# Blocks of eight tokens in place of a scan over 512: the recurrent layers of a four-layer kernel on one core

## The reference

```python
def step(s, rkvw):                      # s is 16 x 16 for each head
    r_t, k_t, v_t, w_t = rkvw
    a = k_t[..., :, None] * v_t[..., None, :]
    out = jnp.einsum('bhi,bhij->bhj', r_t, u * a + s)
    s = a + w_t[..., :, None] * s
    return (s, out)
...
_, out = jax.lax.scan(step, s0, rkvw)   # over 512 tokens
m = og.mean(-1, keepdims=True)          # og: out by heads
va = ((og - m) ** 2).mean(-1, keepdims=True)
og = ((og - m) / jnp.sqrt(va + 1e-05)).reshape(b, l, e) * gn_w + gn_b
x1 = x + og * g @ Wo.T
```

## Time and profile before

| | us |
|---|---|
| median of 3 runs | 4790.81 (4787.45 to 4797.15) |
| the profiled execution, its own time | 4800.18 |
| its span, first to last instruction | 4798.4 |
| TensorE matmul busy | 3797.2 |
| VectorE busy | 3378.0 |
| ScalarE busy | 2119.3 |
| GpSimd busy | 2302.9 |

### The profile page before, as it was taken

The page is one execution under the profiler, slowest core; times in us unless marked ns, Lnnn a source line. Parts: engine busy times, 40 slices in busy tenths (PEclk is TensorE's granted clock), DMA queues, the critical chain, the costliest instruction groups (busy, mean ns, idle before and its releaser), DMA issues. The chain is left out here.

```text
span 4798.4 us, 50379 instructions
## 1 busy us (share of the span) xinstructions
PE 3797.2 (79%) x15616; PEld 2145.1 (45%) x15616; DVE 3378.0 (70%) x5559; ACT 2119.3 (44%) x4624; POOL 2302.9 (48%) x2245
## 2 busy tenths in 40 slices
PE   7888976867888897686788889768668888877766
PEld 4455732424545573252454546234245454623424
DVE  5677379697667738969665773896966577388696
ACT  5576422413657732231365773223137477322313
POOL 4544455354454545535345454543534544454363
PEclk9999977888999998788899999878889999987888
DMA  3123111101212311110121221011022122201102
GB/s 124 39 80 88 53 44 44 44 27 70 70 42 75 88 53 44 49 39 27 70 70 46 74 85 61 36 53 35 27 76 67 49 75 80 77 20 53 35 27 79
DMA packets 95226, 275.38 MB, mean 57 GB/s; under 512 B 25936, under 2 KB 26704, under 8 KB 73808
## 3 DMA queue, kind: packets, MB, share of 16 engines
q1 hardware_dynamic: 94928, 271.84, 17.7%
HBM read 201.49 MB, written 4.19 MB: 43 GB/s over the span
## 5 line engine op out<-in xcount | busy, mean ns | idle before, releaser
L1282 POOL TENSOR_TENSOR prod<-state,rT 128x512 f32<-128x512 f32 x512 | 698.2, 1367 | 662.1 <-DVE state L1060 605.3
L775 POOL TENSOR_SCALAR probs<-probs,row_inv 128x512 f32<-128x512 f32 x1024 | 693.7, 694 | 639.5 <-DVE row_inv L690 639.5
L1060 DVE TENSOR_TENSOR_SCAN state<-decay,s,kvp 128x512 f32<-128x512 f32 x512 | 911.6, 1782 | 12.7 <-POOL prod L1282 12.7
L634 ACT ACTIVATE probs<-probs,row_max 128x512 f32<-128x512 f32 x1024 | 733.3, 725 | 131.2 <-DVE row_max L706 130.0
L529 PE MATMUL ps<-ident,probs 128*128 128x128 f32 x4096 | 605.4, 289 | 172.2 <-ACT pT L628 145.6
L529 PEld LDWEIGHTS ps<-ident,probs 128*128 128x128 f32 x4096 | 476.7, 146 | 382.5 <-ACT pT L628 209.6
L339 PE MATMUL ps<-mix,wring 128*128 128x512 f32 x1024 | 591.6, 677 | 4.8 <-DMA wring<-in_blocks_dram 4.8
L1197 ACT ACTIVATE state<-s 128x1 f32<-128x1 f32 x512 | 102.0, 202 | 1062.2 <-POOL prod L1282 1062.2
L906 PE MATMUL ps<-vstack,pick 128*128 128x512 f32 x512 | 373.7, 732 | 177.0 <-DVE kvp L1052 177.0
L628 ACT ACTIVATE pT<-ps 128x512 f32<-128x512 f32 x768 | 429.8, 603 | 107.8 <-PE ps L529 107.2
L504 PE MATMUL ps<-kstack,qstack 96*128 96x512 f32 (+1 forms) x1024 | 381.6, 467 | 16.8 <-DMA qstack<-hi 7.0
(11 more groups left out here) (142 smaller groups left out, 6526.2 us busy)
## 6 DMA issues: line engine op xcount, KB each, us to landing
wring<-in_blocks_dram SPq DMA_DIRECT2D x151, 1024.0 KB, 5.0
qstack<-hi SPq DMA_DIRECT2D x256, 64.0 KB, 2.0
kstack<-hi SPq DMA_DIRECT2D x256, 64.0 KB, 2.0
maskA<-in_mask_dram SPq DMA_DIRECT2D x9, 1024.0 KB, 7.5
rows<-in_rows_dram SPq DMA_DIRECT2D x8, 1024.0 KB, 4.5
qstack<-hi SPq DMA_DIRECT2D x256, 32.0 KB, 2.0
qstack<-lo SPq DMA_DIRECT2D x128, 64.0 KB, 2.0
kstack<-lo SPq DMA_DIRECT2D x128, 64.0 KB, 2.0
```

Source lines behind the costliest of these rows:

```text
L634: nc.scalar.activation(p, p, ACT.Exp, bias=row_max[:, n % PSLOTS, qc:qc + 1], scale=-1.0, accum_out=row_sum[:, n % PSLOTS, qc:qc + 1]).the ...
L775: nc.gpsimd.tensor_scalar(p, p, row_inv[:, (n - 1) % PSLOTS, qc:qc + 1], 1.0, ALU.mult, ALU.mult)\
L1060: nc.vector.tensor_tensor_scan(state[:, u % 3, 1:L + 1], decay[:, ug, :], kvp[:, u % 3, :], s0[:, ug, uj:uj + 1], ALU.mult, ALU.add)\
L1282: nc.gpsimd.tensor_tensor(prod[:, t % PRODS, :], state[:, t % 3, 0:L], rT[:, hg % 2, :], ALU.mult)\
```

## The change

The 512-step scans are replaced by blocks of 8 tokens. Inside a block the pairs of tokens (earlier s, later t) are handled in levels of 1, 2 and 4: at each level r and k are first multiplied by the decays that lie between (`k2`, `r2`, `k4`, `r4`, `k8`), the products r*k of a pair are summed over a head by a matmul with `head_sum` (`pair_sums`), multiplied by v on VectorE (`bonus`) and added into the output bank through a matmul with `centre`, which takes the mean over the head away. Per block, `fresh_state` forms sum k v on TensorE, 64 matmuls of 32x32 weights and 128 columns for each group; `other` and `states` bring it to SBUF as [P, 64 blocks, 16]; 16 scans over 63 blocks give the state at each block's start. `spread` writes these states block-diagonally (half of the heads on ScalarE, half on VectorE, in two halves of the tokens), and `from_state` multiplies them by r, 64 matmuls of 32 columns of weights and 128 columns. The values are centred when they are turned to tokens, so the output needs no centring. Variance, power, weight and gate are done for each group while the next one is in work; the power (`inverse_root`) is on GpSimd, 128x512 elements for each group. `wo` accumulates group by group in four banks.

```diff
-                    nc.vector.tensor_tensor(kvp[:, t % 3, :], kT[:, hg % 2, :], ps[:, t % 4, :], ALU.mult)
-                    nc.vector.tensor_tensor_scan(state[:, u % 3, 1:L + 1], decay[:, ug, :], kvp[:, u % 3, :],
-                                                 s0[:, ug, uj:uj + 1], ALU.mult, ALU.add)
...
-                nc.gpsimd.tensor_tensor(prod[:, t % PRODS, :], state[:, t % 3, 0:L], rT[:, hg % 2, :], ALU.mult)
...
+            for hg in range(C):
+                values_to_tokens(hg)
+                pair_sums(hg, 0)
+                pair_sums(hg, 1)
+                middle(hg, 0)
+                if hg > 0:
+                    tokens_to_y(hg - 1)
+                pair_sums(hg, 2)
+                keys_to_tokens(hg)
+                if hg > 0:
+                    variance(hg - 1)
+                fresh_state(hg)
+                pair_sums4(hg)
+                bonus_low(hg)
+                middle(hg, 1)
+                bonus_high(hg)
+                tile = from_state(hg, 0, None)
+                middle(hg, 2)
+                from_state(hg, 1, tile)
+            wo(0)
+            tokens_to_y(C - 1)
+            wo(1)
+            variance(C - 1)
+            gate(C - 1)
+            wo(2)
+            wo(3)
...
+            def fresh_state(hg):
...
+                for tc in range(C):
+                    for r in range(4):
+                        rows_ = slice(32 * r, 32 * r + 32)
+                        for q in range(4):
+                            out = ps[32 * q:32 * q + 32, r, :].rearrange('p (two t x) -> p two t x', two=2, t=C)[:, :, tc, :]
+                            m = nc.tensor.matmul(out, k_tok[rows_, tc, 32 * q:32 * q + 32],
+                                                 v_blocks[rows_, tc, q, :, :, :].rearrange('p two b j -> p two (b j)'),
+                                                 start=True, stop=True)
...
+            def from_state(hg, half, tile):
...
+                for tc in (2 * half, 2 * half + 1):
+                    for b4 in range(4):
+                        for q in range(4):
+                            g32 = 4 * tc + q
+                            m = nc.tensor.matmul(tile[32 * q:32 * q + 32, tc * P:(tc + 1) * P],
+                                                 r_blocks[:, 512 * b4 + 32 * g32:512 * b4 + 32 * g32 + 32],
+                                                 state_bd[:, 4 * g32 + b4 - NB // 2 * half, :],
+                                                 start=(b4 == 0), stop=(b4 == 3), skip_group_check=True)
...
+                for j in range(HS):
+                    ins = nc.vector.tensor_tensor_scan(entry[:, 1:NB, j], w8[:, hg, 0:NB - 1], fresh[:, 0:NB - 1, j],
+                                                       s0c[:, hg, j:j + 1], ALU.mult, ALU.add)
...
+            for hg in range(C):
+                pair_products(hg)
+                for level in range(3):
+                    bonus(hg, level)
+                if hg > 0:
+                    variance_out(hg - 1)
+                bonus(hg, 4)
+                states(hg)
+                spread(hg, 0)
+                if hg > 0:
+                    normalise(hg - 1)
+                if hg == C - 1:
+                    gated(0)
+                spread(hg, 1)
...
+            def inverse_root(hg):
+                pool.wait_ge(*dve_emptied.when('var', l, hg))
+                power = rstdT[:, :].rearrange('p (a b) -> p a b', b=32)
+                nc.gpsimd.tensor_tensor(power, power, minus_half[:, :].unsqueeze(1).to_broadcast([P, L // 32, 32]), ALU.pow)\
+                    .then_inc(*pool_done.reach('rstdT', l, hg))
+
+            for hg in range(C):
+                decays(hg)
+            for c in range(C):
+                add_xa('g', c)
+            for hg in range(C):
+                first_entry(hg)
+                if hg > 0:
+                    inverse_root(hg - 1)
             pool_w(pool, f'o_{l}')
+            inverse_root(C - 1)
             pool_w(pool, f'fk_{l}')
```

More of the change, by code:

```diff
@@ L180, in build @@
-    prod, at = place('prod', [P, PRODS, L], at)
-    recT, at = place('recT', [P, C, L], at)
-    assert over <= at
-    gT, at = place('gT', [P, C, L], at)
[L184 to L189, removed]
+    low_z = at
+    ffn_w, at = place('ffn_w', [P, 2, 2, C * H], at, F32R)
@@ L853, in pe_rwkv, with gate @@
                 mixing('g', c)
[L855 to L862, removed]
+            y_bank = ps[:, OBANK, :]
+            def gate(c):
+                if c == 0:
                     w_wait(pe, f'g_{l}')
-                tile = take(pe, 'gp', l, c) if fc == 0 else tile
-                to_T(pe, tile, weights(f'g_{l}'), mix[:, MIX_AT['g']], c, fcs=(fc,),
-                     fin=tile_ready.reach('gp', l, c) if fc == C - 1 else None,
+                to_T(pe, take(pe, 'gp', l, c), weights(f'g_{l}'), mix[:, MIX_AT['g']], c, fin=tile_ready.reach('gp', l, c),
@@ L867, in gate @@
                      ready=(lambda fc: mix_wait(pe, l, 'g', fc)) if c == 0 else None)
-                return tile
[L870 to L883, removed]
@@ L896, in pe_rwkv @@
[L896 to L921, removed]
@@ L922, in pe_rwkv, with values_to_tokens @@
[L922 to L931, removed]
+            def values_to_tokens(hg):
+                pe.wait_ge(*act_emptied.when('vp', l, hg))
+                tile = take(pe, 'vt', l, hg)
+                for tc in range(C):
+                    m = nc.tensor.matmul(tile[:, tc * P:(tc + 1) * P], vT[:, hg % 2, tc * P:(tc + 1) * P], centre[:, :],
+                                         start=True, stop=True)
+                m.then_inc(*tile_ready.reach('vt', l, hg))
@@ new lines, in pair_sums, with pair_sums4 @@
+            def pair_sums(hg, level):
+                if level == 0 and hg > 0:
+                    pe.wait_ge(*dve_done.when('fresh', l, hg - 1))
+                pe.wait_ge(*dve_done.when('rk', l, hg, level))
+                bank, src = ((0, rk0[:, :]), (1, rk1[:, :]), (2, rk2[:, :, :, :]))[level]
+                nc.tensor.matmul(ps[:, bank, 0:256 if level == 1 else 512], head_sum[:, :], src, start=True, stop=True)\
+                    .then_inc(*tile_ready.reach('sums', l, hg, level))
+            def pair_sums4(hg):
+                pe.wait_ge(*dve_done.when('rk', l, hg, 4))
+                for part in range(2):
+                    nc.tensor.matmul(take(pe, 'sums4', l, hg, part), head_sum[:, :], rk4[:, 2 * part:2 * part + 2, :, :],
+                                     start=True, stop=True).then_inc(*tile_ready.reach('sums4', l, hg, part))
@@ new lines, in bonus_low @@
+            def bonus_low(hg):
+                if hg > 0:
+                    pe.wait_ge(*act_done.when('yT', l, hg - 1))
+                pe.wait_ge(*dve_emptied.when('sums', l, hg, 2))
+                nc.tensor.matmul(y_bank, centre[:, :], rk0[:, :], start=True, stop=False, skip_group_check=True)
+                nc.tensor.matmul(y_bank.rearrange('p (b two) -> p b two', two=2)[:, :, 1], centre[:, :], rk1[:, :],
+                                 start=False, stop=False, skip_group_check=True)
+                by4 = y_bank.rearrange('p (b two t) -> p b two t', two=2, t=2)
+                for s in range(2):
+                    m = nc.tensor.matmul(by4[:, :, 1, :], centre[:, :], rk2[:, s, :, :], start=False, stop=False,
+                                         skip_group_check=True)
+                m.then_inc(*S['context_ready'].reach('low', l, hg))
@@ new lines, in bonus_high @@
+            def bonus_high(hg):
+                by8 = y_bank.rearrange('p (b two t) -> p b two t', two=2, t=4)
+                for s in range(4):
+                    if s % 2 == 0:
+                        pe.wait_ge(*dve_emptied.when('sums4', l, hg, s // 2))
+                    m = nc.tensor.matmul(by8[:, :, 1, :], centre[:, :], rk4[:, s, :, :], start=False, stop=False,
+                                         skip_group_check=True)
+                m.then_inc(*S['context_ready'].reach('high', l, hg))
@@ new lines, in wo @@
+            def wo(fc):
+                if fc == 0:
+                    parts_wait(pe, f'o_{l}')
+                    pe.wait_ge(*dve_done.when('fresh', l, C - 1))
+                pe.wait_ge(*dve_done.when('gated_lo', l, fc))
+                for tc in range(C):
+                    for k, (w, x_) in enumerate(three(w_parts(f'o_{l}'), (act_hi[:, 2], act_lo[:, 2]))):
+                        m = nc.tensor.matmul(ps[:, tc, :], x_[:, fc, tc * P:(tc + 1) * P], w[:, fc * H:(fc + 1) * H],
+                                             start=(fc == 0 and k == 0), stop=(fc == C - 1 and k == 2), skip_group_check=True)
+                    if fc == C - 1:
+                        m.then_inc(*tile_ready.reach('wo', l, tc))
@@ new lines, in value_blocks @@
+            def value_blocks(hg):
+                act.wait_ge(*tile_ready.when('vt', l, hg))
+                if hg > 0:
+                    act.wait_ge(*S['fresh_ready'].when(l, hg - 1))
+                for b4 in range(4):
```

(14 more changed lines are left out.)

489 lines of the change are left out of this document (290 added, 199 removed).

## The result

The changed kernel takes 6784.35 us (median of 4 runs, 6765.55 to 6789.4). The kernel before took 4793.98 us beside it (4 runs, 4787.45 to 4810.35). The ratio is 1.4137, 95% interval 1.4092 to 1.4183: slower by 41%, where I had forecast 4% faster. The profiled execution has a span of 6763.7 us against 4798.4.

What follows compares the result with a forecast made beforehand. VectorE was taken to set a stretch's first 160 us, a serial chain the last 26. Groups 141, tail 12.3, power 8 and wait 2 made 163.3 us against 186.7; eight stretches saved 202 us, giving 4590, range 4450 to 5130.

Steps and rivals of the forecast that it cites:

- W: Time of GpSimd's power in inverse_root on 128x512 elements, four times a layer; taken as 8 us, called the unknown.
- The upper bound's reading of the row: The one-element power row's extra 0.36 us paid for each of 512 elements, giving 183 us for the power.
- the power is long: Rival, slower, chance 0.25: GpSimd's power takes long and VectorE's wait exposes it; decides from 14.3 us.
- Its slope: Each us of power above 8 us costs 4 us a stretch: three middle groups and the tail.
- the 7.4 of the prediction: VectorE's PSUM-reading work behind variance_out, 7.4 us, that covers the power before two-input scans wait for GpSimd.
- the 14.8: Cover of the power up to the normalising if VectorE did not wait: 7.4 + 5.3 + 2.1 = 14.8 us.
- break-even: Length of the power from which the change stops paying, forecast at 14.3 us.
- S: Mean stretch, first head product to first add of wo, in each of 4 samples x 2 layers; forecast 163.3 us.
- four at once: fresh_state's small matmuls run side by side in sets of four, 3.6 us; 0.9 us were all sixteen tiles concurrent.
- the prediction's own line: VectorE's cost by elements, through 128 at 0.292 us and 1024 at 1.226: 1.04 ns an element, 0.16 us fixed.
- Small matmuls bound by their issue: Rival, slower, chance 0.10: fresh_state and from_state cost 38 us at 0.148 us a matmul instead of 7.2; 5570 us.
- Better than forecast: Rival, chance 0.07: a power of 1.45 us and sixteen tiles at once give S = 144, 4435 us.

Runs made afterwards that it cites:

- Experiments 2: The changed kernel with the power on 256 of a tile's 512 elements only, the other half keeping its variance: 5468.74 us.
- experiment 3: The changed kernel with the power on the first 128 of a tile's 512 elements only, the rest without its root: 4810.61 us.
- experiment 7: The kernel of experiment 6 plus a GpSimd power on 128x160 elements, whose result nothing reads, at the start of each head group: 4489.01 us.
- experiment 4: The changed kernel with plain GpSimd products for the power: four of 128x2048 in groups 0 and 1, one of 128x512 in the others: 4631.85 us.
- Experiment 1: The changed kernel with a plain product in place of the power on 128x512 elements, the root left out: 4470.66 us.
- experiment 6: The changed kernel with ScalarE's square root and VectorE's reciprocal in place of GpSimd's power, same function: 4466.74 us, ratio 0.9311 to the kernel before.

## Why the prediction was wrong

**The step that failed is W.** The prediction took 8 us for the power on 128x512 between bounds of 1.45 and 183, "nearer the product, the row of the same shape and engine". It is 82.15 us. The one row that showed a power had 0.36 us more than a scalar operation on one element. I argued that a start paid once would explain it. Experiments 2 and 3 show that the power is paid for every element, at 0.160 us, a bit under half of that 0.36. The upper bound's reading of the row was off by a factor of two, mine by ten. The 0.36 itself took the scalar operation at its fastest (0.190 us); its median in the same row is 0.391, the power's 0.548, and 512 times that difference of 0.157 is 80 us. How near that comes may be chance: 0.3 + 0.160 us would be 0.46 for one element, and it took 0.548. It was the operation's own row; the product's row shared only engine and shape. The rival that was named for it, *the power is long*, is what happened, at a size beyond the W = 25 at which the range stopped.

**Its slope was right.** Each us of power costs 4 us a stretch: 4.0 from experiment 3 to 2 and 4.0 from there to the changed kernel. For three of the four the prediction's reason was another than the one found (next paragraph), so that part was luck. By the prediction's own sum W = 82.15 gives 163.3 + 4 x 74.15 = 459.9 us a stretch; 434.7 was measured.

**How the power is exposed was half wrong.** The prediction let VectorE's scans wait until the power ends. They ran through it, 0.326 us each in the changed kernel, and experiment 7 shows it again with nothing that reads the result. The exposure comes from the order instead: VectorE reaches `normalise` 10.9 to 12.4 us after the power begins (once 14.0) and waits there for a semaphore, with the second spread and TensorE behind it. The cover is therefore 11 to 12 us a group and not the 7.4 of the prediction, nearer the 14.8 that it gave for the case without that wait. That is part of why break-even is at 20.2 us and not at 14.3. What the prediction had read in the earlier trace rows held in the changed kernel too: under a plain GpSimd subtraction of 4.50 us a two-input VectorE instruction took 4.98 us.
```profile
983.25 4.50 POOL L321 TENSOR_TENSOR ffn_w<-wring,ffn_w 128x2048 fp32r<-128x2048 f32 x1
983.32 4.98 DVE L1218 SCALAR_TENSOR_TENSOR yn<-yT,cols,rstdT 128x512 f32<-128x512 f32 x1 [71.24 <-POOL rstdT L1473]
```
The subtraction here (4.98 us instead of 0.75) and the products of experiment 4 (a scan of up to 3.76 us instead of 0.33) hold VectorE up; the power, which reads SBUF as well, does not (no scan over 0.352 us). Whether it is the operation or its broadcast exponent that makes the difference isn't shown: the products of experiment 4 had no broadcast input, and beside the product of experiment 1, which had the power's operands, no VectorE instruction ran.

**The rest of the sum was near.** Experiment 1 measures it: S = 146.5 with a product of 1.27 us, where the prediction has 163.3 - 8 - 2 + 1.3 = 154.6. Its parts:
- the first group 29.7 us in the mean (forecast 37), the next two 30.2 and 29.2 (33.7)
- most of those 4 us: sixteen scans in 3.96 us (5.3), a half spread on ScalarE in 2.56 (3.1, twice), `fresh_state` in 1.90 (3.6)
- the last group with the tail 57.4 us (33.7 + 3 + 12.3 + 1.3 = 50.3), forecast 7.1 too low. The sum had 3 us there for GpSimd's subtraction falling on a spread. It falls on two other VectorE instructions, a gating product for 5.02 us (0.75 alone) and an `act_lo` for 4.57 (0.69), 8.2 us more in all
- VectorE 91.6 us a stretch in the changed kernel and 101.0 with experiment 6's four reciprocals of 3.35 us, so 87.6 without them (forecast 87 to 90), of which GpSimd's subtraction holds instructions up for 8.5 and 4.8 us; TensorE 133.0 and 126.7 us (above 125)
- `fresh_state`: 1.90 us for its 128 recorded matmuls in groups 1 to 3 of the changed kernel's first stretch, 2.81 in group 0; the sum had 3.6 with four at once and 0.9 with sixteen. `from_state`: 1.96 and 1.95 us for a half of 64 at a granted clock of 1.00 (1.8), 3.64 at 0.50
- the sum's 0.9 us for a product of 512 columns was the author's estimate. In the earlier trace rows the recorded loads stand 0.43 us apart, two for a product; in the changed kernel's first stretch projections of four products took 3.60 and 3.70 us at a granted clock of 1.00 (line 356), 0.90 and 0.93 us each
- the four tiles of `wo`: from the first add to the last 5.5 us instead of 8.2, 2.7 less (1.9)

Two terms of VectorE's work don't follow from the prediction's own line (eight spreads at 0.51 us are 4.1 and not 4.3, four sums at 0.43 are 1.7 and not 1.9). That is 0.4 us a group and changes nothing.

*Small matmuls bound by their issue* is out: the two take 1.90 + 1.96 + 1.95 = 5.8 us, or 7.5 with one half at a granted clock of 0.50, where that rival decides from 13.5. *Better than forecast* (S = 144) is what the change gives without its power: S = 146.5 and 4470.7 us in experiment 1, 4466.7 in experiment 6.

**The clock.** Forecast at or above 0.83 in the stretches; it was 0.66 with the power, in which TensorE stands still for 64 to 72 us in each of three groups and for 84.1 in the tail, and 0.94 to 0.98 in experiment 6, above the 0.77 to 0.83 of the earlier trace rows. A part of experiment 6's gain may come from that; no run separates it. The half of `from_state` took 3.64 us at a granted clock of 0.50 against 1.96 at 1.00, 1.86 times as long.

## What to carry to other kernels

When the unknown price is that of an operation and not of a shape, take the row of the operation, at one element if there is no other, and multiply its excess by the elements before taking the row of the right shape with another operation; a price between bounds a hundredfold apart calls for a range that reaches to where the nearest row of the operation points. A root on an idle engine isn't free if an in-order engine waits for it in the middle of its list: look at what stands behind the wait (VectorE stood idle for 2361 us ahead of `yn` in the changed kernel). Here a table load and a square root on ScalarE and a reciprocal on VectorE, 5.3 us in all and most of it beside other work, turn a change of +41% into one of -7%.

## What the runs showed of the hardware

- A power on GpSimd costs 0.160 us an element of a partition: 20.78, 41.23 and 82.15 us for 128, 256 and 512. A product on the same 512 costs 1.27 us.
- While it runs, VectorE's two-input instructions are not made to wait for its end (scans 0.326 us, 0.24 to 0.27 us from start to start), though under GpSimd's products they are (up to 3.76 us).
- A reciprocal of 128x512 on VectorE takes 3.35 us, where a product of that shape takes 0.69 to 0.75. A square root of it on ScalarE takes 0.63 us behind a table load of 1.28.
